# A top-k attention kernel: the settling path as a loop, and the memory weights taken inside a merge stage

## The reference

```python
# setup: x (1, 2048, 128); 16 heads of 64, 16 memory keys and values per head, K = 64
# first layer: linear attention with phi(t) = elu(t) + 1, layer norm, top-2 of 8 LoRA experts, layer norm
# the part around the change (second layer's attention; n = 2048 rows):
q = (x @ Wq) per head;  k, v = split(x @ Wkv) per head
k = concat([mem_k, k]);  v = concat([mem_v, v])            # j = n + 16 columns
dots = einsum('bhid,bhjd->bhij', q, k) * 64 ** -0.5
dots = einsum('bhij,hk->bkij', dots, pre_proj)             # heads are mixed
dots = where(causal, -inf, dots)
thresh = top_k(dots, 64)[0][..., -1:]                      # 64th largest of each row
dots = where(dots < thresh, -inf, dots)
out = einsum('bhij,bhjd->bhid', softmax(dots), v) @ Wo + bo
# then layer norm, a top-1 mixture of 8 experts with a shared expert, layer norm
```

## Time and profile before

| | before |
|---|---|
| median of 3 runs | 3034.04 us (3031.94 to 3041.01) |
| the profiled execution: its own time | 3029.58 us |
| its span, first to last instruction | 3027.1 us |
| granted TensorE clock, mean | 0.859 of full speed |
| the groups: start of the first and the last line 1119 | 329.7 and 2684.4 us |

### The profile page before, as it was taken

One profiled execution on the slowest core, in us unless ns is written; L12 is line 12 of the kernel. 1 busy time (PEld: TensorE's weight loads), 2 busy tenths in 40 slices (PEclk: granted clock), 3 DMA queues, 4 the chain that ended last, 5 costly groups with the idle time before them and its releaser, 6 DMA issues.

```text
span 3027.1 us, 34365 instructions
## 1 busy us (share of the span) xinstructions
PE 2302.1 (76%) x10182; PEld 1328.8 (44%) x10182; DVE 2415.8 (80%) x9392; ACT 1414.6 (47%) x2143; POOL 5.2 (0%) x43
## 2 busy tenths in 40 slices
PE   6696545657767757778888888988984888884897
PEld 3554323333434424444444444544542545442564
DVE  2506688889888988989899999999998988884445
ACT  1121223444445435555565666666663666652221
POOL 0000000000000000000000000000000000000000
PEclk7798667777878878899998999999997999987898
DMA  2000000000000000000000000000000000001000
GB/s 59 1 0 1 1 1 1 1 1 1 2 1 1 1 1 1 1 1 1 1 1 1 1 1 1 1 1 1 1 1 1 1 1 1 1 1 49 1 1 14
DMA packets 15509, 12.20 MB, mean 4 GB/s; under 512 B 6892, under 2 KB 13686, under 8 KB 15222
## 3 DMA queue, kind: packets, MB, share of 16 engines
q1 hardware_dynamic: 11184, 6.82, 0.9%
q10 hardware_dynamic: 4038, 2.37, 0.3%
HBM read 8.14 MB, written 1.05 MB: 3 GB/s over the span
## 4 chain that ended last, share of the span: by engine, by line
DVE 53%; PE 30%; ACT 8%; issue 7%; DVEq 2%; ACTq 0%
DVE cand L1106 13%; DVE R L1155 7%; DVE r L1157 7%; PE bank L823 6%; PE bank L791 6%; PE bank L903 4%; DVE W L1136 4%; DVE F L1176 4%; DVE W L1135 4%; ACT R L543 4%; PE bank L807 3%; ACT R L536 3%; PE bank L911 2%; DVE WP L1170 2%; PE bank L808 1%
## 5 line engine op out<-in xcount | busy, mean ns | idle before, releaser
L823 PE MATMUL bank<-WP,Y 128*128 128x512 f32 x1088 | 685.4, 718 | 152.0 <-ACT WP L550 151.2
L807 PE MATMUL bank<-ident,R 128*128 128x128 f32 x2176 | 524.0, 315 | 248.8 <-ACT R L543 246.6
L1106 DVE MAX8 cand<-R 128x8 f32<-128x12 f32 (+15 forms) x4096 | 642.6, 226 | 5.3 <-ACT R L521 4.2
L791 PE MATMUL bank<-hT,qT 128*128 128x512 f32 (+3 forms) x1280 | 533.1, 555 | 37.3 <-ACT R L521 22.2
L807 PEld LDWEIGHTS bank<-ident,R 128*128 128x128 f32 x2176 | 346.2, 159 | 465.6 <-issue 214.7
L550 ACT ACTIVATE WP<-bank 128x512 f32<-128x512 f32 x544 | 320.8, 594 | 369.8 <-PE bank L808 368.6
L808 PE MATMUL bank<-nidentb,F 128*128 128x128 bf16 x2176 | 466.3, 240 | 0.0
L536 ACT ACTIVATE R<-R,cutb 128x144 f32<-128x144 f32 (+15 forms) x256 | 310.2, 1212 | 294.1 <-DVEq L1148 292.5
L521 ACT ACTIVATE R<-bank 128x1024 f32<-128x1024 f32 (+7 forms) x384 | 290.5, 774 | 278.6 <-PE bank L791 168.3
L1155 DVE SCALAR_TENSOR_TENSOR R<-R,r 128x144 f32<-128x144 f32 (+15 forms) x256 | 350.3, 1368 | 9.2 <-DVE r L1154 0.2
L543 ACT ACTIVATE R<-R,negm 128x144 f32<-128x144 f32 (+15 forms) x256 | 289.8, 1205 | 123.9 <-DVEq L1254 123.7
(11 more groups left out here) (225 smaller groups left out, 2164.1 us busy)
## 6 DMA issues: line engine op xcount, KB each, us to landing
R<-in_L_attn_Wkv ACTq DMA_DIRECT2D x2, 512.0 KB, 8.0
R<-in_L_ffn_gate_w SPq DMA_DIRECT2D x1, 1024.0 KB, 7.7
R<-in_L_ffn_up_w SPq DMA_DIRECT2D x1, 1024.0 KB, 10.3
out<-X SPq DMA_DIRECT2D x1, 1024.0 KB, 5.1
R<-in_L_attn_Wq ACTq DMA_DIRECT2D x1, 512.0 KB, 6.1
WP<-in_L_attn_Wo ACTq DMA_DIRECT2D x1, 512.0 KB, 10.5
R<-in_L_ffn_wi SPq DMA_DIRECT2D x1, 256.0 KB
R<-in_L_ffn_wo SPq DMA_DIRECT2D x1, 256.0 KB
```

The costliest lines, as they stand in the source:

```text
L791: last = pe.matmul(to, qT[:, k % 2, i, :], hT[:, a:b], start=True, stop=b < n, skip_group_check=True)
L807: pe.transpose(to[:, P * i:P * i + P], S[:, k % NS, i, blk], ident[:, :])
L823: pe.matmul(bank[6], Y[:, j, :], PT[:, (blocks_before(k) + j) % 4, :], start=(j == 0), stop=(j == k // 4))\
L1106: mark(dve.max(cand[:, :, c, i], lists(S[:, k % NS, i, 0:n], n, c)))
```

## The change

Two things are changed, both on VectorE. The first is the settling code: it now finds the doubt of all four units at once, then goes through the units in a loop of four turns and through the first seven rounds of the 64-largest search in an inner loop. A doubtful row is first copied to scratch, since the rounds of a loop must all read the same tile. The branch in front of it now jumps 38 instructions ahead, counted as above, and 37 of these are the settling code. The second: `memory_weights(k - 1)` is called inside `beside`, in merge stage 5 + k // 16 (5 for groups 1 to 15, 8 for groups 48 to 63), behind the four MAX8 of that stage; the call between `pivots` and `below` is gone.

```diff
--- before.py
+++ after.py
@@ -201,7 +201,7 @@
         full = sb("full", [P, 2])
         doubt = sb("doubt", [32, 4 * GU])
         doubts = sb("doubts", [32, 2, 32])
-        flag = sb("flag", [1, 1], mybir.dt.int32)
+        flag = sb("flag", [1, 1 + GU], mybir.dt.int32)
         rden = sb("rden", [P, GU])
         bob = sb("bob", [P, P])
         ident = sb("ident", [P, P])
@@ -1112,6 +1112,8 @@
                     mark(ins)
                     stage = done[0]
                     list_step(k + 1, 4 * step, 4)
+                    if k >= 1 and step == 5 + k // 16:
+                        memory_weights(k - 1)
                     dve.wait_ge(s_dve, stage)
                     return step + 1
 
@@ -1175,27 +1177,38 @@
                 n = wide(k // 4)
                 mark(dve.tensor_scalar(F[:, i, 0:n], S[:, k % NS, i, 0:n], thr[:, i:i + 1], 4.0, ALU.is_lt, ALU.mult))
 
-            def settle(k, i):
+            def settle(k):
+
 
                 n = wide(k // 4)
-                dve.tensor_reduce(doubts[:, 0, 0:1], doubt[:, i::GU], AX.X, ALU.max)
+                rest, eight = A[:, 1, 0:n], r9[:, 0, 1:9]
+                dve.drain()
+                dve.tensor_reduce(doubts[:, 0, 0:GU], doubt[:, :].rearrange("p (g i) -> p i g", i=GU), AX.X, ALU.max)
                 dve.drain()
                 dve.transpose(doubts[:, 1, :], doubts[:, 0, :])
                 dve.drain()
-                dve.tensor_reduce(flag[:, :], doubts[0:1, 1, :], AX.X, ALU.max)
+                dve.tensor_reduce(doubts[:, 0, 0:1], doubts[:, 1, :], AX.X, ALU.max)
                 dve.drain()
-                row, rest, m_ = S[:, k % NS, i, 0:n], A[:, 1, 0:n], r9[:, i, 1:9]
-                with dve.If(dve.value_load(flag[0:1, 0:1], min_val=0, max_val=1) != 0):
-                    for r in range(8):
-                        dve.max(m_, rest if r else row)
+                dve.transpose(doubts[:, 1, :], doubts[:, 0, :])
+                dve.drain()
+                dve.tensor_copy(flag[:, 1:1 + GU], doubts[0:1, 1, 0:GU])
+                dve.drain()
+                with dve.Fori(0, GU) as i:
+                    row = R[:, bass.ds(i * WIDE + (k % NS) * GU * WIDE, n)]
+                    with dve.If(dve.value_load(flag[0:1, bass.ds(i + 1, 1)], min_val=0, max_val=1) != 0):
+                        dve.tensor_copy(rest, row)
                         dve.drain()
-                        if r < 7:
-                            dve.match_replace(rest, m_, rest if r else row, 2 * FILL)
+                        with dve.Fori(0, TOPK // 8 - 1):
+                            dve.max(eight, rest)
                             dve.drain()
-                    dve.tensor_copy(thr[:, i:i + 1], m_[:, 7:8])
-                    dve.drain()
-                    dve.tensor_scalar(F[:, i, 0:n], row, thr[:, i:i + 1], 4.0, ALU.is_lt, ALU.mult)
-                    dve.drain()
+                            dve.match_replace(rest, eight, rest, 2 * FILL)
+                            dve.drain()
+                        dve.max(eight, rest)
+                        dve.drain()
+                        dve.tensor_copy(thr[:, bass.ds(i, 1)], eight[:, 7:8])
+                        dve.tensor_scalar(F[:, :, :].rearrange("p i n -> p (i n)")[:, bass.ds(i * WIDE, n)], row, eight[:, 7:8],
+                                          4.0, ALU.is_lt, ALU.mult)
+                        dve.drain()
 
             def threshold(k):
                 t = k // 4
@@ -1241,15 +1254,13 @@
                 judged = done[0]
                 mask(k, 2)
                 dve.wait_ge(s_dve, judged)
-                mark(dve.tensor_reduce(flag[:, :], doubts[0:1, 1, :], AX.X, ALU.max))
+                mark(dve.tensor_reduce(flag[:, 0:1], doubts[0:1, 1, :], AX.X, ALU.max))
                 judged = done[0]
                 mask(k, 3)
                 dve.wait_ge(s_dve, judged)
                 doubtful = dve.value_load(flag[0:1, 0:1], min_val=0, max_val=1)
                 with dve.If(doubtful != 0):
-                    dve.drain()
-                    for i in range(GU):
-                        settle(k, i)
+                    settle(k)
                 dve.wait_ge(s_dve, done[0])
                 dve.sem_inc(s_lose, 1)
 
@@ -1263,8 +1274,6 @@
             list_step(0, 0, CH * GU)
             for p in range(NG):
                 pivots(p)
-                if p >= 1:
-                    memory_weights(p - 1)
                 for i in range(GU):
                     below(p, i)
                 threshold(p)
```

## The result

The changed kernel takes 3079.4 us (median of 4 runs, 3078.89 to 3080.83) against 3034.38 us (4 runs of the kernel before beside it, 3031.94 to 3041.01). The ratio is 1.0146, with a 95% interval of 1.0128 to 1.0163: slower by 45 us, where 53.5 was forecast. The profiled execution took 3078.91 us, its span 3077.2.

The account below looks back on a forecast made before the run. VectorE was taken to lead up to group 30, then the loop over ScalarE and TensorE. -38.3 - 2.3 + 8 + 52.1 + 5.2 + 23.8 + 5 = +53.5 us on 3034 gave 3088 us, own range 3055 to 3115.

Parts of the forecast that it names:

- The loop that Pm closes: Groups 31 to 62: early Pm waits for exponents, delaying cut and counts; +52.1 us to group 54, +23.8 in 57 to 62.
- TensorE's clock: Behind the first counts of groups 32 to 43: longer distances go with a lower granted clock, +5 us (0 to +30).
- The gaps: VectorE in front of line 1119: all 38 long gaps go; -38.3 us up to group 30, -2.3 us behind group 63.
- The settling path: Doubtful groups 26 and 55: looped settling code costs +4 us each, +8 us in all (-2 to +18).
- the refetching rival: Settling loop: each jump back costs a long gap's 2.25 us, 20 of them add 45; about 3128 us, chance 6%.
- the +5.2 of its wait: Group 55: the cut comes 8.9 us after the exponents instead of 2.36, +5.2 us after the mask's spare time.
- no gap over 1.5 us: Sign in the profile after: VectorE has no idle gap above 1.5 us in front of line 1119.
- TensorE works ahead: Rival: same loop, but TensorE uses the longer wait, each group 1.5 us shorter; 3053 us, chance 15%.
- The gaps stay: Rival: long gaps do not depend on jump length, so the -40.6 us don't come; 3129 us, chance 7%.
- The wait stays hidden: Rival: exponents catch up, the cut is no link of the loop, only gains are left; 2972 us, chance 10%.
- The marks along the way: Signs: group 31 starts about 35 to 41 us earlier, group 50 about level, group 63 about 45 to 50 later.

Follow-up runs that it names:

- Stages 15, 11 and 5: Changed kernel with Pm taken in merge stage 15 or 11 from group 31 on, or 5 in all groups: 2955.47, 2961.86 and 3163.89 us.
- the loop alone: Changed kernel with Pm back in its old place behind the cut, so only the settling code differs from the kernel before: 2956.76 us, ratio 0.9740.
- behind `below`: Settling loop as changed, with Pm taken behind the second unit of below, later than in its old place: 2949.3 us, ratio 0.9724.
- jump 102: Settling loop with Pm in its old place, padded with 64 drains inside the branch, which then jumps 102 instructions: 2967.17 us, ratio 0.9779.
- jump 166: Settling loop with Pm in its old place, padded with 128 drains inside the branch, which then jumps 166 instructions: 3020.09 us, ratio 0.9947.

## Why the prediction was right

**The loop that Pm closes.** Right, and in size. The 24 distances of groups 31 to 54 add up to 213.7 us (216.0 forecast, 163.9 before), so +49.8 for +52.1. Groups 57 to 61 gave +19.5 for +20.0, group 62 +3.7 for +3.8. What follows a first count in group 60 took 40.0 us, as it had the earlier trace rows. Stages 15, 11 and 5 show it as cause: the time follows the distance, not VectorE's wait.

**TensorE's clock.** The excess behind the first count was put at +5 us in groups 32 to 43 and came to +12.0 in groups 31 to 54, all of it in 32 to 47. The granted clock of the middle stretch is 0.90, where it was 0.93; the sign was right, the size too small. In all ten traces the two go together: from first count to next exponents groups 32 to 47 need 433 to 436 us where the granted clock of these pieces is 0.99 to 1.00 (the loop alone, Pm at stages 15 and 11, behind `below`, and jump 102), 438.5 at 0.97 (before), 442.0 at 0.97 (jump 166), and 450 to 452 at 0.90 to 0.91 (Pm at stages 5 to 8). No experiment changes the clock alone, so that it is the cause, and not only a companion of the longer wait, stays argued.

**The gaps.** Forecast -38.3 us and +4 for settling group 26 up to T31; measured -51.9 in all. The term was mis-sized by some 15 us, for four reasons. The long gaps were counted one short: the trace of before has 38 among the 63 rows and one more behind the last group, and 18 of them, not 17, lie between T1 and T31 (the window of the earlier trace rows ends at 1240 us, ahead of the gap in front of group 31): 2 us. The largest part is that the prediction took all short gaps for one size. Two rows after, behind the branches of groups 24 and 25:

```profile
978.89 0.27 DVE L1121 TENSOR_REDUCE top<-cand 128x4 f32<-128x64 f32 x1 [0.69 <-DVE F L1178]
...
1010.75 0.27 DVE L1121 TENSOR_REDUCE top<-cand 128x4 f32<-128x64 f32 x1 [0.38 <-DVE F L1178]
```

The 0.38 is a jump inside a packet, which a jump of 206 can't be. Behind 20 of groups 1 to 30 the jump saves this 0.33, 7 us. Another 4 us are stalls of 0.8 to 1.6 us within the merges of groups 4, 11 and 18 that the trace of before has and the new one hasn't. Group 4, before, on VectorE:

```profile
418.61 0.42 DVE L1120 TENSOR_SCALAR W<-cand 128x512 f16<-128x512 f32 x1
420.65 0.29 DVE L1128 TENSOR_TENSOR W<-W 128x256 f16<-128x256 f16 x1 [1.62 <-issue]
```

In these three groups the jump had ended near the end of a packet. The next packet starts 0.5 us behind line 1119, and the stalled instruction 1.7 to 1.9 us behind the packet's start; in the long gaps it is 1.9 from the packet's start to line 1119. So it looks like the same wait for code, a few instructions later. The last 2 us are 0.08 us a group in which VectorE's own work between the gaps got shorter. That the short jump is the cause of the gaps' going is shown by the padded kernels.

**The settling path.** Forecast +4 us for each. Measured +1.9 in group 26, and +8.5 in group 55, where +4 and the +5.2 of its wait were forecast. Group 26 after, on VectorE:

```profile
1043.09 0.16 DVE L1194 CAST flag<-doubts 1x4 int32<-1x4 f32 x1
1044.35 0.63 DVE L1199 COPY R<-R 128x912 f32 x1 [1.10 <-issue]
1045.13 1.11 DVE L1202 MAX8 r<-R 128x8 f32<-128x912 f32 x1
1046.32 0.09 DVE L1204 MATCH_VALUE_LOAD R<-r,R 128x8 f32 x1
1046.40 1.09 DVE L1204 MATCH_REPLACE8 R<-r,R 128x912 f32<-128x912 f32 x1
1047.88 1.11 DVE L1202 MAX8 r<-R 128x8 f32<-128x912 f32 x1 [0.39 <-issue]
...
1065.33 0.69 DVE L1209 TENSOR_SCALAR F<-R,r  x1
...
1069.92 0.27 DVE L1121 TENSOR_REDUCE top<-cand 128x4 f32<-128x64 f32 x1 [3.90 <-issue]
```

A jump back costs 0.39 us from one round to the next, where straight code has below 0.1: within the 0 to 0.5 that was given, and far from the 2.25 of the refetching rival, which is thereby out. The Trainium skill ("Advanced Engine Details and Errata", Control Flow Timing) has about 0.11 us for a compare and branch; the row shows some 0.3 for the jump of a counted loop, which has a register instruction beside it. The three units without doubt behind the doubtful one take the 3.90 us of the last row, which is an exception to "no gap over 1.5 us".

**The rivals.** TensorE works ahead: the distance from a first count to the next exponents didn't shrink (712.2 us for 700.2), so no. The gaps stay: no. The wait stays hidden: not with Pm at these stages; it is what happens at stage 15, and there the time is 2955 us. The marks along the way: group 31 starts 43.8 us earlier (35 to 41 forecast), group 50 1.0 later ("about level"), group 63 51.1 later (45 to 50). These look close because of the 8.4 us in front of the first group. Counted from T0 they are 52.2 earlier, 7.4 earlier and 42.7 later, so the early gain was larger and the balance at the end smaller than forecast. VectorE waits 172.7 us for the exponents (150 forecast), none of it up to group 30 and 7.9 of it behind the last group.

**The sum.** Between the two profiled executions it is +49.3 us, with 8.4 of it in front of the first group; so the groups give +41, where +53.5 was forecast. The gaps bring 15 us more, the clock takes 7 more, and the distances and the settling make up the rest. That these two errors have opposite signs is luck, and so part of the closeness of the total is; the loop's term, the largest, was right by itself. The medians stand 45.0 apart.

## What to carry to other kernels

On an engine that works in order, ask of a moved instruction what it waits for and who waits for what stands behind it, size by size: the same place was free in 30 groups and cost 3.7 us in each of the last ones, since the producer ends later there. The price is what the way round the loop gains in length, not the wait that the profile shows, and a wait on an engine with time to spare (TensorE's 130.9 us for Pm) may be worth nothing. Code that is nearly always skipped should be short, here below 128 instructions, best in the same packet as its branch. And two edits that go together should be timed apart: here one was worth -79 us, the other +89, and only the sum was seen.

## What the runs showed of the hardware beyond that

- A forward jump on VectorE has three prices here (groups 1 to 30) by where it lands: 1.05 us from the last mask (load and branch within) in the same packet of 8.2 KB, 1.36 to 1.45 in the next, 3.6 to 3.9 two ahead. In the last case one packet of the instruction queue starts within the gap, 38 times of 38, and in the others none does.
- A counted loop's jump back costs some 0.3 us and fetches nothing again: in group 26 the instruction queue moves no packet from 1044.5 to 1066 us.
- Identical instructions ahead of the first group took 328.9 to 340.5 us in ten executions. This spread of 11.6 us is more than the 6.4 us between stages 11 and 15. Two single executions can be compared only from T0 on.
